# Four reorderings in a one-core transformer kernel: clip order, item numbers on another engine, a last tile in halves, early activations

## The reference

```python
x = x + L0_xattn(ln(x), ctx);      x = x + L0_ffn(ln(x))          # two local-attention layers, gelu
x = x + L1_xattn(ln(x), ctx)       # softmax(q k^T, causal) v
x = x + L1_ffn(ln(x))              # softmax router, top 2 of 8 experts, capacity 320, shared silu hidden
x = x + L2_xattn(ln(x), ctx, ctx)  # 16 heads of 16, softmax(QK^T/4) V, output projection, biases
x = x + L2_ffn(ln(x))              # x, h and weights rounded to 8 bits: clip(round(v/scale), -128, 127)*scale
x = x + L3_xattn(ln(x), ctx, ctx)  # 16 heads, position bias, mask, e / (1 + sum e)
x = x + L3_ffn(ln(x))              # top 2 of 8 experts, softmax over the two logits, silu, none dropped
```

## Time and profile before

| | us |
|---|---|
| median of 3 runs (lowest to highest) | 1524.14 (1523.89 to 1527.91) |
| the profiled execution | 1522.96 |
| its span | 1521.2 |

### The profile page before, as it was taken

One profiled execution on the slowest core, in us unless ns is written; L12 is line 12 of the kernel. 1 busy time (PEld: TensorE's weight loads), 2 busy tenths in 40 slices (PEclk: granted clock), 3 DMA queues, 4 the chain that ended last, 5 costly groups with the idle time before them and its releaser, 6 DMA issues. The chain is left out here.

```text
span 1521.2 us, 28369 instructions
## 1 busy us (share of the span) xinstructions
PE 1345.9 (88%) x9297; PEld 1060.1 (70%) x9298; DVE 984.3 (65%) x2633; ACT 762.4 (50%) x1817; POOL 534.6 (35%) x625
## 2 busy tenths in 40 slices
PE   6878999999999999999999898979956799569993
PEld 4656887777887887887887656857644377459992
DVE  4357677667777777777776466459868589543223
ACT  1224655556556556556556644127756566223331
POOL 3332222222222223233232215726663544235551
PEclk9979999999999999999999999999988599879997
DMA  8000000000000100000000454362010000111224
GB/s 332 19 1 1 1 1 1 0 1 0 1 28 1 39 1 1 0 0 0 0 1 1 171 234 152 122 241 99 1 43 7 1 1 1 56 42 65 69 64 172
DMA packets 29790, 74.96 MB, mean 49 GB/s; under 512 B 7799, under 2 KB 13192, under 8 KB 27900
## 3 DMA queue, kind: packets, MB, share of 16 engines
q1 hardware_dynamic: 22876, 55.63, 9.9%
q0 software_dynamic: 6816, 18.14, 3.8%
HBM read 54.41 MB, written 20.88 MB: 49 GB/s over the span
## 5 line engine op out<-in xcount | busy, mean ns | idle before, releaser
L1152 PE MATMUL banks<-l_ffn_in_wqkv,l_ffn_hT 128*128 128x512 f32 x384 | 178.3, 601 | 0.0
L1235 PE MATMUL banks<-l_ffn_h2T,l_ffn_in_w 128*128 128x128 f32 x1408 | 175.7, 277 | 0.0
L1235 PEld LDWEIGHTS banks<-l_ffn_h2T,l_ffn_in_w 128*128 128x128 f32 x1408 | 167.0, 192 | 7.3 <-issue 5.7
L1364 ACT ACTIVATE l_ffn_work<-l_ffn_work,l_ffn_att_bias 128x256 f32<-128x256 f32 x256 | 126.4, 495 | 70.5 <-DVE l_ffn_att_bias L1520 70.5
L1393 ACT ACTIVATE l_ffn_gate<-banks,l_ffn_layer_cols 128x128 f32<-128x128 f32 x160 | 51.7, 364 | 184.0 <-PE banks L1235 170.8
L1086 POOL TENSOR_TENSOR l_ffn_rden_wide<-l_ffn_att_rden,ones 128x512 f32<-128x512 f32 x32 | 33.2, 1038 | 251.0 <-DVE l_ffn_att_rden L1531 251.0
L1152 PEld LDWEIGHTS banks<-l_ffn_in_wqkv,l_ffn_hT 128*128 128x128 f32 x384 | 68.1, 190 | 71.7 <-issue 71.6
L1243 PE MATMUL banks<-l_ffn_in_w,l_ffn_ff 128*128 128x256 f32 (+1 forms) x384 | 104.6, 389 | 0.0
L1091 POOL TENSOR_TENSOR l_ffn_rstd<-l_ffn_ve,neg_half 128x1 f32<-128x1 f32 x32 | 20.0, 625 | 208.6 <-DVE l_ffn_ve L1557 208.6
L3282 POOL TENSOR_TENSOR L__probs<-L__probs,L__rec 128x1024 f32<-128x1024 f32 x32 | 60.9, 1902 | 86.2 <-DVE L__rec L3237 86.2
L1401 ACT ACT_TABLE_LOAD x68 | 87.2, 1283 | 1.2
(11 more groups left out here) (460 smaller groups left out, 3298.3 us busy)
## 6 DMA issues: line engine op xcount, KB each, us to landing
l_plan_rows<-l_plan_pairs SPq DMA_DIRECT2D x16, 512.0 KB, 7.4
l_ffn_in_w<-in_L_w SPq DMA_DIRECT2D x2, 4096.0 KB, 17.6
l_ffn_in_down<-in_L_down SPq DMA_DIRECT2D x1, 4096.0 KB, 13.2
l_plan_pairs<-l_plan_rows SPq DMA_DIRECT2D x4, 1024.0 KB, 17.0
l_plan_table<-l_plan_rows SPq DMA_DIRECT2D x8, 512.0 KB, 2.9
l_ffn_in_wqkv<-in_L_wqkv SPq DMA_DIRECT2D x1, 3072.0 KB, 16.3
l_ffn_in_w<-in_L_w SPq DMA_DIRECT2D x4, 640.0 KB, 14.6
x_res<-in_x SPq DMA_DIRECT2D x4, 512.0 KB, 5.5
```

The source lines that it names most:

```text
L1152: mm = pe.matmul(ps[:, (Q, K, V)[n], :], hT[:, m.b, m.odd, ch, 1 - ch:P + 1 - ch], wqkv[:, bass.ds(m.layer, 1), ch, n * INNER:(n + 1) * IN ...
L1235: mm = pe.matmul(ps[:, HIDDEN[pair], to:to + P], w1[:, ch, at:at + P], h2T[:, ch, m.b, :], start=(j % 2, n, ch) == (0, 0, 0), stop=ch == D ...
L1364: ex = nc.scalar.activation(work[:, m.b, slot, :], work[:, m.b, slot, :], ACT.Exp, bias=bias[:, m.b, slot:slot + 1], scale=-1.0, accum_out ...
```

## The change

1. Routing, both uses: the logits are no longer copied to SBUF; reductions and comparisons read PSUM. The product of flags and item numbers (was L1930) moves from VectorE to GpSimd as `item_numbers`, in two halves behind the partition-number product. in_row is written in four parts (PARTS). In the first routing the five instructions that finish the weights move behind in_row. The bank of places is read in place, but for one copy of the item half.
2. attend_and_route: the Silu activations of h = 0, 1 and 2 stand in ScalarE's turns 9, 10 and 11, and an exponential of one column behind the turns; UP_TO_SUMS is 8, so that product 7 stands ahead of the sums.
3. cross_attention: for the last tile (LAST) maxima, subtraction, exponential, denominators, transposes and copies run in two halves of 8 heads; the subtraction follows the maxima in the same step; GpSimd multiplies the first half, VectorE the second. On TensorE the last tile's transposes stand ahead of the projection of the tile before. For all tiles VectorE's add stands ahead of the statistics.
4. Down product: in each step VectorE's clip stands ahead of scaled_out and stats.

```diff
@@ class Routing
+    PARTS = 4
     def places(self, pe):
         for i in range(ITEMS):
             if i % (ITEMS // 2) == 0:
-                pe.wait_ge(s.placed.sem, s.placed.at(0, i // (ITEMS // 2) + 1))
+                pe.wait_ge(s.ones_set.sem, s.ones_set.at(0, i // (ITEMS // 2) + 2))
+            if i % (ITEMS // self.PARTS) == 0:
+                pe.wait_ge(s.placed.sem, s.placed.at(0, i // (ITEMS // self.PARTS) + 3))
+    def item_numbers(self, p):
+        s, of_item = self.e.s, expert_constants()[1][2]
+        p.wait_ge(s.placed.sem, s.placed.at(0, 2))
+        for half in range(2):
+            own = slice(half * ITEMS // 2, (half + 1) * ITEMS // 2)
+            p.tensor_tensor(self.place[:, own, 1, :], self.in_tile[:, own, :],
+                            self.const[:, of_item][:, own].unsqueeze(2).broadcast_to((P, ITEMS // 2, self.n_tiles)), ALU.mult).then_inc(s.ones_set.sem, 1)
@@ assign
-        v.tensor_tensor(self.place[:, :, 1, :], self.in_tile[:], self.const[:, of_item].unsqueeze(2).broadcast_to((P, ITEMS, self.n_tiles)), ALU.mult)
-        for half in range(2):
-            own = slice(half * ITEMS // 2, (half + 1) * ITEMS // 2)
-            v.tensor_tensor(self.in_row[:, own, :], self.low[:, own].unsqueeze(2).broadcast_to((P, ITEMS // 2, P)),
-                            self.const[:, to_p].unsqueeze(1).broadcast_to((P, ITEMS // 2, P)), ALU.is_equal).then_inc(s.placed.sem, 1)
+        v.wait_ge(s.placed.sem, s.placed.at(0, 1))
+        v.tensor_scalar(self.place[:, :, 0, :], self.in_tile[:], given.p_col[:], None, ALU.mult).then_inc(s.placed.sem, 1)
+        wide = ITEMS // self.PARTS
+        for part in range(self.PARTS):
+            own = slice(part * wide, (part + 1) * wide)
+            v.tensor_tensor(self.in_row[:, own, :], self.low[:, own].unsqueeze(2).broadcast_to((P, wide, P)),
+                            self.const[:, to_p].unsqueeze(1).broadcast_to((P, wide, P)), ALU.is_equal).then_inc(s.placed.sem, 1)
@@ attend_and_route
-    UP_TO_SUMS = 7
+    SILU_AT = {9: 0, 10: 1, 11: 2}
+    UP_TO_SUMS = 8
@@ its ScalarE turns
+                if n in SILU_AT:
+                    silu(SILU_AT[n])
+            nc.scalar.activation(attention.less_mean[:, 0:1], e.zero_eps[:, 0:1], ACT.Exp)
             routing.exponents(act_, TILES)
-            for h in range(ALL_TILES):
+            for h in range(len(SILU_AT), ALL_TILES):
+                silu(h)
@@ cross_attention, TensorE
                 def step(behind):
                     behind(queries, 2)
+                    behind(lambda m: probs_transposed(m) if m.n == LAST else None, 4)
                     behind(projected, 5)
-                    behind(probs_transposed, 4)
+                    behind(lambda m: None if m.n == LAST else probs_transposed(m), 4)
@@ cross_attention, VectorE
                 def denominators(m):
+                    for h in halves(m):
...
+                        if h == 1:
+                            v.wait_ge(s.rden_ready.sem, done(s.rden_ready, m.n, h))
+                            v.tensor_tensor(probs[:, m.b, own, :], probs[:, m.b, own, :],
+                                            rec[:, m.b, own].unsqueeze(2).broadcast_to((P, HALF_XH, CTX)), ALU.mult).then_inc(s.mix_ready.sem, 1)
                 def step(behind):
-                    behind(subtract, 3)
+                    behind(lambda m: None if m.n == LAST else subtract(m), 3)
+                    behind(add, 5)
+                    behind(lambda m: denominators(m) if m.n == LAST else None, 3)
                     behind(stats, 6)
-                    behind(add, 5)
-                    behind(denominators, 3)
+                    behind(lambda m: None if m.n == LAST else denominators(m), 3)
                     behind(maxima, 2)
@@ l2_ffn, VectorE's step of the down product
+                    if three:
+                        clip(three)
                     if one:
                         scaled_out(one)
                     stats(zero)
-                    if three:
-                        clip(three)
```

More of the change, by code:

```diff
@@ new lines, in assign @@
+        if self.dropping:
+            dve.link(v.scalar_tensor_tensor(self.comb[:], self.rank[:], float(CAPACITY), self.comb[:], ALU.is_le, ALU.mult))
+            dve.link(v.tensor_reduce(self.weight[:], self.comb[:], AX.X, ALU.add))
+            dve.link(v.tensor_scalar(self.weight[:], self.weight[:], 1e-6, None, ALU.add))
+            dve.link(v.reciprocal(self.weight[:], self.weight[:]))
+            dve.link(v.tensor_tensor(self.comb[:], self.comb[:], self.weight[:].unsqueeze(2).broadcast_to((P, ALL_TILES, E8)), ALU.mult))
+        else:
@@ L2213, in _ @@
                 attention.rstd(p, pool, n)
+            routing.item_numbers(p)
         @block.tensor
@@ L3059, in cross_attention, with halves, heads, done @@
         CQ, MO, SCORES, PROBS_T = 0, 1, 2, 6
+        begin(1, s.mix_ready)
+        LAST = ALL_TILES - 1
+        IN_HALVES = (LAST,)
+        in_halves = (s.max_ready, s.probs_ready, s.rden_ready, s.probsT_psum, s.probsT_ready)
+        begin(1, *in_halves)
+        def halves(m):
+            return (0, 1) if m.n in IN_HALVES else (None,)
+        def heads(h):
+            return slice(0, XH) if h is None else slice(h * HALF_XH, (h + 1) * HALF_XH)
+        def done(signal, n, h=None):
+            if n < 0:
+                return signal.base
+            return signal.base + n + 1 + sum(t < n for t in IN_HALVES) + (n in IN_HALVES and h != 0)
         def each_tile(step):
@@ L3227, in subtract @@
[L3227 to L3237 removed]
+                    v.wait_ge(s.probsT_psum.sem, done(s.probsT_psum, m.n - BATCH))
@@ new lines, in subtract @@
+                    for h in halves(m):
+                        of = scores_of(m, h)
+                        v.wait_ge(dve.sem, found[m.n, h])
+                        v.tensor_tensor(probs[:, m.b, heads(h), :], of, top[:, m.b, heads(h)].unsqueeze(2).broadcast_to(of.shape), ALU.subtract)\
+                         .then_inc(s.max_ready.sem, 1)
+                def denominators(m):
+                    for h in halves(m):
+                        own = heads(h)
+                        v.wait_ge(s.probs_ready.sem, done(s.probs_ready, m.n, h))
+                        dve.link(v.tensor_reduce(den[:, m.b, own], probs[:, m.b, own, :], AX.X, ALU.add))
+                        if sink:
+                            dve.link(v.tensor_scalar(den[:, m.b, own], den[:, m.b, own], 1.0, None, ALU.add))
+                        v.wait_ge(s.scaled.sem, s.scaled.before(m.it, m.k))
+                        v.reciprocal(rec[:, m.b, own], den[:, m.b, own]).then_inc(s.rden_ready.sem, 1)
+                        if h == 1:
+                            v.wait_ge(s.rden_ready.sem, done(s.rden_ready, m.n, h))
+                            v.tensor_tensor(probs[:, m.b, own, :], probs[:, m.b, own, :],
+                                            rec[:, m.b, own].unsqueeze(2).broadcast_to((P, HALF_XH, CTX)), ALU.mult).then_inc(s.mix_ready.sem, 1)
```

131 lines of the change are left out of this document (67 added, 64 removed).

## The result

| | before | changed |
|---|---|---|
| median, us (15 runs each) | 1524.14 | 1519.57 |
| lowest to highest | 1519.94 to 1528.14 | 1514.41 to 1525.05 |
| ratio to before, with 95% interval | | 0.9971 (0.9960 to 0.9983) |
| profiled execution, its span | 1522.96, 1521.2 | 1521.86, 1520.0 |

The change takes off 4.4 us (2.6 to 6.1), 0.29%. The forecast was 6.3 (0.41%), the time 1517.8; the measured one lies inside the range, at the edge of what a measurement tells from none. Medians of the kernel before move by up to 14 us from chip to chip, and two executions of one kernel on one chip by up to 12; all ratios are to the kernel before on the same chip.

What follows compares the result with a forecast made beforehand. The prediction saw a serial relay between engines in five places; routing -1.8 and +0.5, down product -2.5, cross attention ends -1.1 and -1.4 sum to -6.3 us, median 1517.8 from 1524.14, range 1514.6 to 1521.0.

Runs made afterwards that it cites:

- base: The kernel before, run again with no edit for a second trace; one execution, 1534.71 us on a chip with median 1537.03 for this kernel.
- again: The changed kernel, run again with no edit for a second trace; ratio to before 0.9965 (0.9948 to 0.9983).
- no_halves: Changed kernel with the last tile of both cross attentions whole again, the add still ahead of the statistics; ratio to before 0.9963 (0.9941 to 0.9985).
- warm: Kernel best plus unused TensorE work: 24 transposes ahead of the quantised layer's gate and up, 26 products behind the second cross attention; ratio to before 0.9948.
- best: Changed kernel with last routing's row numbers read from PSUM and, in both cross attentions, tile 14's statistics ahead of the last add; 1514.20 us, ratio 0.9938.

## What to carry over

When an edit moves work to GpSimd, or puts GpSimd beside VectorE, look at the operands: two operands in SBUF on VectorE's side made a product moved to GpSimd 0.6 us dearer than on VectorE, and a row of constants copied to PSUM made it 1.4 cheaper. An instruction's duration in a profile holds its neighbours: in its new place the clip took 0.56 and 0.99, not the 0.76 it had. And a difference of 0.3% in a kernel whose executions spread by 0.5 to 0.8% is proved by stretches between marks on one engine, in at least two traces of each kernel, not by its time. An effect that such stretches show still needs its cause tested: here the table itself spoke against the first explanation of C.

## What the runs showed of the hardware

- VectorE and GpSimd hold each other one instruction at a time, tiny ones too: the addition of 128x2 took 0.51 when it was issued inside the clip and 0.19 otherwise; the power of 128x1 0.87 and 0.55. The clip took 0.42 more than what was left of GpSimd's addition to x when it was issued (0.99 with 0.58 left, 0.77 with 0.35), 0.56 where that addition was over, and 0.50 with GpSimd idle.
- An operand of VectorE in PSUM removed the hold wholly (four comparisons 4.61, alone 4.62), and itself cost nothing.
- Behind a pause, the same products at the same moment can run at the lower of TensorE's two levels (0.50, 1.2 GHz) for longer in one trace than in another: C is 29.66 in base, 30.47 in again and 31.00 in no_halves. Of the eleven traces of changed kernels without filling products, C is longer than in both of before in all, G in ten, F in nine (the other two have 3.81 against 3.80) and I in eight. A shorter stage in front doesn't explain it, since no_halves has longer ones (B 31.05, E 18.81) and loses too; what does stays open.
- At the change of stages an engine waits for the queues of the others, TensorE's with work that nobody needs included (2.21 us of waiting in the kernel warm, where in best VectorE waits 0.94 for GpSimd's last power and no longer).
